# Two low-rank layers on one core: two blocks share one product with G, and ScalarE, VectorE and TensorE work in another order

## What is computed

```python
def _L0_cond_ref(x, adapter_ids, base_weight, base_bias, lora_A_w, lora_B_w):
    result = jnp.einsum('bsd,od->bso', x, base_weight) + base_bias
    A = lora_A_w[adapter_ids]
    Bw = lora_B_w[adapter_ids]
    h = jnp.einsum('bsd,brd->bsr', x, A)
    return result + jnp.einsum('bsr,bor->bso', h, Bw)

def _L1_cond_ref(x, A, B, adapter_ids):
    Bx = jnp.einsum('bni,bri->bnr', x, B[adapter_ids])
    return jnp.einsum('bnr,bor->bno', Bx, A[adapter_ids])

x = x + _L0_cond_ref(x, itok_B_6_15, ...)
x = x + _L1_cond_ref(x, L1_cond_A, L1_cond_B, itok_B_3_7)
```

## Time and profile before

| | |
|---|---|
| median of 3 runs | 98.22 us (97.8 to 98.43) |
| the profiled execution | 97.73 us, span 96.0 us from the first to the last instruction |
| granted clock of TensorE | 0.996 of full speed |
| busy: TensorE, VectorE, ScalarE, GpSimd | 91.3, 64.3, 60.9, 57.9 us |
| DMA | 19.38 MB, 202 GB/s over the span |

### The profile page before, as it was taken

One profiled execution on the slowest core, in us unless ns is written; L12 is line 12 of the kernel. 1 busy time (PEld: TensorE's weight loads), 2 busy tenths in 40 slices (PEclk: granted clock), 3 DMA queues, 4 the chain that ended last, 5 costly groups with the idle time before them and its releaser, 6 DMA issues.

```text
span 96.0 us, 2292 instructions
## 1 busy us (share of the span) xinstructions
PE 91.3 (95%) x652; PEld 89.4 (93%) x652; DVE 64.3 (67%) x121; ACT 60.9 (63%) x191; POOL 57.9 (60%) x126
## 2 busy tenths in 40 slices
PE   5999999999998999999999999999999999999980
PEld 5799999999896999999999999999999999999970
DVE  4659998509016757959586777769595867775470
ACT  3244699855749895958686867758586868671210
POOL 6504067800478999999576584949585766807500
PEclk9999999999999999999999999999999999999998
DMA  2999999946676268999999699992836354520206
GB/s 21 319 399 388 369 326 340 254 106 180 172 173 248 61 231 260 234 266 271 225 219 335 106 320 219 245 250 105 229 49 222 58 188 51 203 109 0 109 0 219
DMA packets 16111, 19.38 MB, mean 202 GB/s; under 512 B 1220, under 2 KB 11332, under 8 KB 15940
## 3 DMA queue, kind: packets, MB, share of 16 engines
q1 hardware_dynamic: 14816, 13.97, 49.4%
q0 software_dynamic: 1280, 5.28, 22.0%
q10 hardware_dynamic: 4, 0.00, 0.0%
HBM read 13.40 MB, written 5.84 MB: 201 GB/s over the span
## 4 chain that ended last, share of the span: by engine, by line
PE 84%; DMA 7%; issue 2%; DVE 1%; POOL 1%; ACT 1%; DVEq 0%; POOLq 0%; SPq 0%
PE psum L394 51%; PE psum L431 11%; PE psum L379 4%; DMA gathered_rows<-by_rank,rows 4%; PE psum L423 4%; PE psum L477 4%; DMA by_rank<-row_ends 3%; PE psum L371 3%; PE psum L363 3%; PE psum L456 2%; PE psum L405 2%; PE psum L439 1%; DVE y L682 1%; POOL g_sel L333 1%; ACT row_ends L555 1%
## 5 line engine op out<-in xcount | busy, mean ns | idle before, releaser
L394 PE MATMUL psum<-wd,xt 128*128 128x256 f32 (+1 forms) x384 | 62.4, 311 | 0.4 <-ACT wd L555 0.2
L394 PEld LDWEIGHTS psum<-wd,xt 128*128 128x128 f32 x384 | 56.3, 188 | 1.0 <-issue 0.9
L555 ACT ACTIVATE wd<-table_rounded 128x128 fp32r x128 | 27.8, 298 | 12.2 <-PE psum L394 10.8
L340 POOL TENSOR_TENSOR up_rows<-gathered_rows,up_rows 128x512 fp32r<-128x512 f32 x16 | 20.6, 1290 | 14.1 <-ACT up_rows L555 14.1
L323 POOL DMA_INDIRECT gathered_rows<-by_rank,rows x16 | 15.9, 995 | 8.4 <-DMA by_rank<-row_ends 5.9
L643 DVE TENSOR_TENSOR xt<-psum,xt 128x512 fp32r<-128x512 f32 x16 | 11.1, 691 | 7.0 <-ACT xt L555 7.0
L650 DVE STREAM_TRANSPOSE psum<-x_squares 128x512 f32<-128x512 f32 x13 | 14.4, 1110 | 0.0
L431 PE MATMUL psum<-up_rows,u_sel 128*128 128x256 f32 x96 | 14.1, 283 | 0.0
L555 ACT ACTIVATE xt<-psum 128x512 fp32r<-128x512 f32 x16 | 9.6, 598 | 5.6 <-DVE psum L650 4.7
L662 DVE STREAM_TRANSPOSE psum<-psum 128x128 f32<-128x128 f32 x16 | 5.3, 330 | 11.4 <-PE psum L394 11.4
L431 PEld LDWEIGHTS psum<-up_rows,u_sel 128*128 128x128 f32 x96 | 12.9, 190 | 0.0
(11 more groups left out here) (63 smaller groups left out, 67.2 us busy)
## 6 DMA issues: line engine op xcount, KB each, us to landing
out<-y SPq DMA_DIRECT2D x15, 256.0 KB, 3.8
x_squares<-in_x SPq DMA_DIRECT2D x8, 256.0 KB, 7.1
w_rows<-in_L_cond_base_weight SPq DMA_DIRECT2D x4, 256.0 KB, 4.6
bw_rows<-in_L_cond_lora_B_w SPq DMA_DIRECT2D x1, 1024.0 KB, 7.1
a_rows<-in_L_cond_lora_A_w SPq DMA_DIRECT2D x1, 1024.0 KB, 10.2
by_rank<-bw_by_rank SPq DMA_DIRECT2D x4, 256.0 KB
x_rows<-in_x SPq DMA_DIRECT2D x3, 256.0 KB, 7.3
x_squares<-in_x SPq DMA_DIRECT2D x12, 64.0 KB, 2.3
```

The lines of the kernel that those rows point to most:

```text
L340: nc.gpsimd.tensor_tensor(out=up_rows[:, k % 2, LO, :], in0=gathered_rows[:, k % GATHERS, 0:D], in1=up_rows[:, k % 2, HI, :], op=ALU.subtr ...
L394: last = nc.tensor.matmul(bank_of(k, half)[:, start:end], xt[:, k % X_SLOTS, c, x_part, :], wd[:, w_part, c, col:col + end - start], start ...
L555: return nc.scalar.activation(dst, src, ACT.Copy)
```

## The change

Blocks 1 to 14 are taken as seven pairs, j = 0 to 6, of the blocks 2j+1 and 2j+2; blocks 0 and 15 stay single. In odd and even blocks the two layers' halves of the 32 rows of a sample lie the other way round (`half_of`), so that layer 0's u of both blocks fit into one 128-row tile u_pair, and one product with g_pair gives both blocks' parts for layer 1. GpSimd writes u_pair as the first block's u_own times a 0/1 mask (`begin_pair`), VectorE adds the second block's (`finish_pair`); after the product VectorE adds each block's part to its u_own (`add_u`, twice, into the new tile u_all in SBUF), from which `u_high` and `u_low` are taken. u_own has two buffers. `u_low` is a scalar_tensor_tensor (1.0 times u less its high half) instead of a tensor_tensor. All queues are written anew in pairs: on TensorE both `up` of a pair are within the next odd block's base product; `xt_high(k)` waits for one `u_filled` more; `select` of the second block follows `u_high`; on SyncE four x loads move ahead, the first of them behind the first gather. In the setup the masks get a third column, two short GpSimd copies, one reduction and one more tensor_scalar on VectorE. The rest is as it was. The diff, cut to the core:

```diff
     for k in range(NBLK - 1):
-        if k in (1, 2, 3, 6):
-            load_x(5 + (1, 2, 3, 6).index(k))
+        if k == 0:
+            sp.wait_ge(gathered[0], 16)
+        if k in (0, 1, 2, 6):
+            load_x(5 + (0, 1, 2, 6).index(k))
         sp.wait_ge(y_ready, k + 1)
...
     def g_select(k):
         n1 = adapters_of(pool, k, L1)
         pool.wait_ge(gathered[k % GATHERS], 16 * (k // GATHERS) + 16)
-        if k >= 2:
-            pool.wait_ge(gh_filled, k - 1)
+        if k not in SINGLES and k >= 5:
+            pool.wait_ge(gh_filled, g_products(k - 4))
         for b in range(NB):
-            last = nc.gpsimd.tensor_tensor(
-                out=g_sel[:, k % 2, b, L1, :], in0=gathered_rows[:, k % GATHERS, bass.ds(n1[b] * R + G_COL, R)],
-                in1=batch_mask[:, b, 0:R], op=ALU.mult)
+            g_row = gathered_rows[:, k % GATHERS, bass.ds(n1[b] * R + G_COL, R)]
+            if k in SINGLES:
+                last = nc.gpsimd.tensor_tensor(out=g_sel[:, k % 2, b, half_of(k, L1), :], in0=g_row,
+                                               in1=batch_mask[:, b, 0:R], op=ALU.mult)
+            else:
+                last = nc.gpsimd.tensor_tensor(
+                    out=g_pair[:, (k - 1) // 2 % 2, b, half_of(k, L1), :], in0=g_row,
+                    in1=rank_mask[:, half_of(k, L0), b:b + 1].to_broadcast([P, R]), op=ALU.mult)
         last.then_inc(g_ready, 1)
...
+    def begin_pair(j):
+        k = 2 * j + 1
+        pool.wait_ge(u_own_ready, k + 1)
+        pool.wait_ge(half_mask_ready, 1)
+        if j >= 1:
+            pool.wait_ge(gh_filled, g_products(k - 1))
+        nc.gpsimd.tensor_tensor(out=u_pair[:, :], in0=u_own[:, k % 2, :],
+                                in1=half_mask[:, half_of(k, L0):half_of(k, L0) + 1].to_broadcast([P, P]),
+                                op=ALU.mult).then_inc(u_pair_begun, 1)
...
-    for k in range(NBLK):
-        g_select(k)
+    g_select(0)
+    up_low(0)
+    g_select(1)
+    gather(3)
+    g_select(2)
+    for j in range(PAIRS):
+        k = 2 * j + 1
+        begin_pair(j)
+        if 1 <= j < PAIRS - 1:
+            gather(k + 3)
         up_low(k)
+        up_low(k + 1)
+        if j == 0:
+            gather(k + 3)
+        if k + 4 < NBLK:
+            gather(k + 4)
+        g_select(k + 2)
         if k + 3 < NBLK:
-            gather(k + 3)
+            g_select(k + 3)
+    up_low(NBLK - 1)
...
+    def pair_gh(j):
+        pe.wait_ge(u_pair_ready, j + 1)
+        pe.wait_ge(g_ready, 2 * j + 3)
+        pe.wait_ge(u_ready, 1)
+        if j >= 1:
+            pe.wait_ge(u_all_ready, 2 * j)
+        nc.tensor.matmul(u_now, g_pair[:, j % 2, :, :, :], u_pair[:, :],
                          start=True, stop=True).then_inc(gh_filled, 1)
...
-    add_gh(1)
-    for k in range(3, NBLK - 1):
+    for j in range(PAIRS - 1):
+        k = 2 * j + 3
         wait_x(k)
         wait_d(k)
         wait_slot(k)
         base(k, [0])
-        if k == 3:
-            up(1)
-            base(k, [1])
-        add_gh(k - 1)
-        base(k, range(2 if k == 3 else 1, C))
+        pair_gh(j)
+        base(k, [1, 2])
+        up(k - 2)
+        base(k, [C - 1])
         up(k - 1)
+        k = 2 * j + 4
+        wait_x(k)
+        wait_d(k)
+        wait_slot(k)
+        for half in (U_AT[k % 2][0], 1 - U_AT[k % 2][0]):
+            base(k, range(C), halves=[half])
...
-    add_gh(k - 1)
+    pair_gh(PAIRS - 1)
     base(k, range(1, C), halves=[d_half])
-    base(k, range(0, C - 1), halves=[other_half])
+    base(k, range(0, 2), halves=[other_half])
+    up(k - 2)
     add_gh(k)
     up(k - 1)
-    base(k, [C - 1], halves=[other_half])
+    base(k, range(2, C), halves=[other_half])
...
-            act.wait_ge(u_filled, k - X_SLOTS + 1)
+            act.wait_ge(u_filled, k - X_SLOTS + 2)
...
-        act.wait_ge(gh_filled, k + 1)
+        if k in SINGLES:
+            act.wait_ge(gh_filled, g_products(k))
+        else:
+            act.wait_ge(u_all_ready, k)
         if k >= 2:
             act.wait_ge(out_filled, k - 1)
-        copy(u_sel[:, k % 2, HI, :], u_now).then_inc(u_hi_ready, 1)
+        copy(u_sel[:, k % 2, HI, :], whole_u(k)).then_inc(u_hi_ready, 1)
...
-    select(3, L0)
-    up_high(1)
-    select(3, L1)
-    u_high(1)
-    up_high(2)
-    for k in range(3, NBLK - 1):
-        select(k + 1, L0)
-        select(k + 1, L1)
-        u_high(k - 1)
-        xt_high(k + 1)
+    for j in range(PAIRS):
+        k = 2 * j + 1
+        select(k + 2, L0)
+        select(k + 2, L1)
+        if j == 0:
+            up_high(k)
+            up_high(k + 1)
+            select(k + 3, L0)
+            select(k + 3, L1)
+            u_high(k)
+            u_high(k + 1)
+            xt_high(k + 3)
+            xt_high(k + 4)
+            continue
+        if k + 3 < NBLK:
+            xt_high(k + 3)
         up_high(k)
-    u_high(NBLK - 2)
+        up_high(k + 1)
+        u_high(k)
+        u_high(k + 1)
+        if k + 3 < NBLK:
+            select(k + 3, L0)
+            select(k + 3, L1)
+            xt_high(k + 4)
...
     def u_low(k):
         dve.wait_ge(u_hi_ready, k + 1)
-        low(u_sel[:, k % 2, LO, :], u_now, u_sel[:, k % 2, HI, :]).then_inc(u_ready, 1)
+        nc.vector.scalar_tensor_tensor(out=u_sel[:, k % 2, LO, :], in0=whole_u(k), scalar=1.0,
+                                       in1=u_sel[:, k % 2, HI, :], op0=ALU.mult, op1=ALU.subtract,
+                                       ).then_inc(u_ready, 1)
+    def finish_pair(j):
+        k = 2 * j + 2
+        dve.wait_ge(u_pair_begun, j + 1)
+        dve.wait_ge(u_own_ready, k + 1)
+        dve.wait_ge(half_mask_ready, 1)
+        nc.vector.scalar_tensor_tensor(out=u_pair[:, :], in0=u_own[:, k % 2, :],
+                                       scalar=half_mask[:, half_of(k, L0):half_of(k, L0) + 1], in1=u_pair[:, :],
+                                       op0=ALU.mult, op1=ALU.add).then_inc(u_pair_ready, 1)
+    def add_u(k):
+        dve.wait_ge(gh_filled, g_products(k))
+        if k >= 3:
+            dve.wait_ge(u_ready, k - 1)
+        nc.vector.scalar_tensor_tensor(out=u_all[:, k % 2, :], in0=u_now,
+                                       scalar=half_mask[:, half_of(k, L1):half_of(k, L1) + 1],
+                                       in1=u_own[:, k % 2, :],
+                                       op0=ALU.mult, op1=ALU.add).then_inc(u_all_ready, 1)
...
-    turn_u(1)
-    own_u(1)
-    finish(0)
-    u_low(1)
-    for k in range(3, NBLK):
-        turn_u(k - 1)
-        own_u(k - 1)
-        finish(k - 2)
-        if k + 1 < NBLK:
-            x_turn(k + 1)
-        u_low(k - 1)
-        if k + 1 < NBLK:
-            xt_low(k + 1)
+    for j in range(PAIRS):
+        k = 2 * j + 1
+        turn_u(k)
+        own_u(k)
+        finish(k - 1)
+        if 1 <= j < PAIRS - 1:
+            x_turn(k + 3)
+        turn_u(k + 1)
+        own_u(k + 1)
+        finish_pair(j)
+        if 1 <= j < PAIRS - 1:
+            xt_low(k + 3)
+        add_u(k)
+        add_u(k + 1)
+        u_low(k)
+        u_low(k + 1)
+        if j == 0:
+            x_turn(k + 3)
+            finish(k)
+            xt_low(k + 3)
+            x_turn(k + 4)
+            xt_low(k + 4)
+        elif j < PAIRS - 1:
+            x_turn(k + 4)
+            finish(k)
+            xt_low(k + 4)
     turn_u(NBLK - 1)
     own_u(NBLK - 1)
+    finish(NBLK - 3)
```

78 lines of the change are left out of this document (52 added, 26 removed).

## The result

| | before | after |
|---|---|---|
| median of 5 runs each, same session | 98.06 us (97.80 to 98.43) | 104.53 us (103.84 to 106.00) |
| ratio | | 1.064 (95% interval 1.058 to 1.069) |
| profiled execution, span | 97.73 us, 96.0 us | 106.00 us, 104.2 us |
| mean granted clock of TensorE | 0.996 | 0.976 |

The change makes the kernel 6.4% slower. The forecast was 99.5 us with a range to 101.2, so the sign was right and the size was not: 1.3 us were expected and 6.5 came. (A ratio leaves out runs more than 1.5% above the fastest of the same kernel, so it need not be the quotient of the medians beside it.)

A forecast was written before the change was run, and what follows sets the result against it. TensorE's own work was taken to bound the kernel. The terms -1.54 + 0.22 + 1.83 + 0.1 + 0.7 gave +1.3 us, so 99.5 us at the median, with a range of 97.3 to 101.2.

The forecast's parts named there:

- the opening's order: First pairs: VectorE's queue order makes TensorE late at four places, together 1.83 us.
- 1.23 late: Opening, second pair's product: done at 45.61 us where TensorE would have had it done at 44.38.
- the tail: End of the kernel: up(15) comes 0.7 us late, since up_high(15) waits for block 13's out_filled.
- the steady chain: Later pairs: dependency chain across engines takes 8.62 us against TensorE's 8.59, losing some 0.1 us over four pairs.
- the price of a new VectorE instruction that runs free: VectorE, each pair: finish_pair and each add_u taken at 0.35 us, with 0.27 as lower bound.
- The half element rate: VectorE's scalar_tensor_tensor with two SBUF inputs: upper bound of 0.49 us each, 0.14 more than 0.35.
- 34.40 to 34.75: Opening, VectorE: start and end forecast for finish_pair(0), a duration of 0.35 us.
- rival 3: VectorE instructions with two SBUF inputs and GpSimd's hold each other up: 101.7 us at most, 100.0 with first part; chance 0.18.
- the price of `u_low` in the later pairs: Later pairs: xt_low about 0.2 us later behind held u_low, plus 0.14 half rate on finish_pair: 0.34 x 5 = 1.7 us.

The follow-up runs named there:

- the probe: The kernel before plus one unneeded 128x128 VectorE tensor_tensor a block, both inputs in SBUF, behind xt_low: 105.48 us, ratio 1.078.

## Why the prediction was right or wrong

**Right: the opening's order.** Of the "1.23 late" at the second product 0.27 is the product itself, which takes 0.49 behind a wait and 0.22 without one; so a wait of 0.96 was forecast and 0.81 to 0.84 measured in the kernels that kept VectorE's order and have no wait of GpSimd for `u_low`. With both locks gone it starts at 45.41 (45.17 with the 0.24 by which that execution ran later) against a forecast 45.12. Moving x_turn (with ScalarE's `up_high`, in one edit) takes the wait away, which fits the cause named.

**Right: the tail.** "0.7 us late" was 0.49, and ordering `up(13)` earlier took it away.

**Right within 0.1 for a pair, and low in the sum: the steady chain.** 8.62 us for a pair were forecast, 8.73 measured with the locks gone. Over five pairs that adds up: in the kernel with no lock left the second product starts at 45.02 (forecast 45.12) and the seventh, on the chain, at 88.78 (88.14). So 0.7 us are lost between them that the forecast doesn't have, 0.1 at each pair and the rest at the sixth product, which takes 0.49 instead of 0.22. That is one part of why this kernel stands at 1.029 and not at the forecast's 1.013; the rest no profile shows, since the profiled execution was the fastest of its four (99.69 against a median of 100.53).

**Right: the price of a new VectorE instruction that runs free.** 0.35 forecast for `finish_pair` and `add_u`, 0.352 and 0.347 measured. Two `u_low` take 0.49 to 0.55 together. The half element rate, 0.49 for one, which I took as the upper end, showed nowhere. The Trainium skill's page "Vector Engine (DVE) Microarchitecture Reference" (points that are easy to get wrong) gives scalar_tensor_tensor with two SBUF sources that aren't bf16 half the throughput. The traces don't agree at this size: 352 ns with both tensors in SBUF (`finish_pair`), 351 with the first in PSUM (`u_own`).

**Wrong: the term for `finish_pair(0)`, "34.40 to 34.75".** The start was right to 0.02 us in the second session, the duration was not: 2.29 to 2.55 for 0.35. The step that failed is in rival 3, where I let the lock fall on `u_low` only. `finish_pair(0)` stands right behind `begin_pair(0)`, and GpSimd's next two instructions are up_low(1) and up_low(2), whose inputs are ready by then, so the two meet. (In pairs 1 to 5 a gather and ScalarE's `up_high` hold the low halves back, and `finish_pair` takes 0.35.) I had put up_low(2) at 35.6 to 36.9, so up_low(1) at about 34.3 to 35.6, and `finish_pair(0)` at 34.40 inside it. The positions were in my working and I did not lay them side by side. Cost: 1.9 us. The Trainium skill's page "SBUF — State Buffer", section on its two separate sides, says that whichever starts first has the shared ports for its whole instruction and the other blocks. The traces agree: 1.39 us for 0.28 beside one low half. In `finish_pair(0)` the wait was for two instructions: 2.55 for 0.35. I had given the rule little because no row of before showed it. But no row spoke against it either, since the kernel before has no such instruction.

**Wrong in its parts, right in the total by luck: the price of `u_low` in the later pairs.** Rival 3 had "0.34 x 5 = 1.7", 0.2 by the lock and 0.14 by half rate. No half rate showed, and the two `u_low` took 1.4 to 1.64 together, 0.8 to 1.1 more than free. From the second product to the seventh, on the chain, the changed kernel takes 45.49 us (second session) and the kernel with no lock left 43.76. So the lock costs 1.7 over the five pairs, 0.35 for each where 0.2 was named for it. The other 0.7 of the 2.5 above are the steady chain's, as just said.

**Wrong: nothing allowed for what comes after a wait.** That the clock would fall in the long wait of TensorE was in no term and in no rival. It adds 1.4 us where it happens, as it did in some executions of the changed kernel and not in others.

**Wrong in the chances.** Rival 3 had 0.18, with 101.7 at most; so the range ended at 101.2. Its cause was the main one. The sum for it, worked with the measured sizes, would have been 1.3 + 1.9 + 2.5 = 5.7, so 103.9 at the median of 98.22, and the nine runs of the changed kernel lie at 101.99 to 106.00.

**What stays open.** How much of the difference between the two sessions (1.064 and 1.043) is the clock and how much the gather's landing, since only one execution of each is profiled. Why the clock fell behind waits of 1.73 and 1.87 us in two kernels and not behind 1.80 in a third. Why `finish_pair(6)` got in between two low halves and `finish_pair(0)` did not. And the 0.05 us that remain of 8.73 against 8.59 when the first `up` is counted.

## What to carry to other kernels

Before adding a VectorE instruction that reads two tensors from SBUF, look up which GpSimd instructions can run at that moment, and price it at their remaining length, up to all that are queued back to back; if it stands on the way to TensorE, keep one operand in PSUM or order GpSimd behind it, and see what else stands in GpSimd's queue. Look first where GpSimd's next instructions have their inputs ready when VectorE is released. And a stall of TensorE of some 2 to 3 us isn't priced at its own length: behind one of 3.09 us the lower clock cost another 1.4.

## What the runs showed of the hardware that I had not expected

- **Two GpSimd instructions back to back can hold a VectorE instruction for both.** `finish_pair(0)` started 0.06 us behind the first and ended 0.14 behind the second (2.55 us; 2.29 in another session). Not always: `finish_pair(6)`, 0.03 behind the first of two, was held for that one alone (1.40), as was the probe beside one low half (1.39).
- **The granted clock falls in mid-kernel with an idle stretch.** Behind an idle time of 3.09 us it stood at 0.50 and 0.60 of full speed for 3.6 us; behind 1.80 us in another profile of the same kernel it stayed at 1.00. It fell also with 1.73, 1.87, 3.22 and 3.53 us in other kernels, and stayed with 1.47.
- **The same kernel scatters once it has such a stall:** 101.99 to 106.00 us over its nine runs, where the kernel before stays within 97.80 to 99.10 in the same two sessions (97.26 to 99.61 over all).
